# A decoder layer on one core: softmax weights of 4 of 50 key tiles made by VectorE as a base-2 polynomial, self masks moved to GpSimd

## Chip, core and metric

The kernel runs on one core of one Trainium2 chip. The metric is the device time of one launch, from the first to the last instruction of all engines, in microseconds (us). Several launches are timed and their median is taken; one more launch is run under the hardware profiler.

## What is computed

One pre-norm decoder layer in fp32: x has 1024 rows of 128, the context has 6404 rows of 96, there are 16 heads of 8 numbers each, and a mixture of 8 experts (2 chosen per row) at the end.

```
x = x + self_attention(layernorm(x))            # causal, 1024 keys, scale 1/sqrt(128)
x = x + cross_attention(layernorm(x), ctx)      # 6404 keys, no mask, scale 1/sqrt(8)
x = x + experts(layernorm(x))                   # 8 x (128->512->128), top 2 by a router
```

In each attention the weights are softmax(q k * scale), so every score needs one exponential: 16 heads x 1024 queries x 6404 keys in the cross attention, 105 million of them. Everything around the change is the making of these exponentials.

## The kernel before, in words

**Tiles.** Keys are taken in tiles of 128, queries in halves of 512, heads in four quads of four heads (lanes, r = 0 to 3). One PSUM bank holds the scores of one head, one key tile and one query half: 128 keys on the partitions, 512 queries. The cross attention has 8 units (2 halves x 4 quads); a unit has 50 key tiles of 4 banks, 200 banks, and a short tail of 4 keys per head whose exponentials are made once in `ptail`. So there are 1600 cross banks.

**Groups.** `score_groups` cuts the list of banks into groups; ScalarE turns a group into softmax numerators with one ACTIVATE (Exp) from PSUM to the slots of `probs` (15 slots of 512). In the self attention (48 groups) and the first 66 groups of the cross attention a group has 3 banks (PSUM banks 0 to 2, then 3 to 5; bank 6 is used for side work). From then on groups have 4 and 3 banks in turn (PSUM banks 0 to 3, then 4 to 6). The cross attention has 467 groups. PSUM is thus double-buffered: the scores of group g+2 go where those of group g lay.

**TensorE's order** is the loop in `attention` (L1252 on). For every group it waits until ScalarE has done the exponentials of that group, writes the scores of group g+2 (`score_group`, L1248), then sums every tile whose four banks are complete by group g: `sum_batch` (L1276) multiplies the weights of the four heads with the values, 4 matmuls of 512 columns that show as 8 in the trace since fp32 takes two passes. All sums of a unit go into PSUM bank 7. At the end of a unit the tail is summed (L1272), VectorE transposes the bank (L895), divides (L899, L902), and the first sum of the next unit waits for that transpose. The instructions of TensorE run in this order only.

**ScalarE's order** is `exponentials` (L659 on): for every group it waits for the scores of the group, and for the sums that still read the slots of `probs` that it will overwrite, then makes the exponentials (L665).

**VectorE** in the self attention multiplies each diagonal block of 128 x 128 weights by a 0/1 matrix `causal` (L916, 128 blocks in 29 of the 48 groups), after the exponentials of the group and before TensorE may sum them; `normalise` places the unit ends and the first half's projection and norm in the same order. In the cross attention after its first unit VectorE has only the unit ends.

**SyncE (SP)** loads key pieces into `k_ring` (five slots; 32 loads of 16 DMAs), each when its slot has been scored. Ahead of load five it issues the two 2 MB loads of the expert weights (L497, L498) into `w1_region` and `ctx_region`; TensorE waits for both at L1465, ahead of the first hidden units (L1499). **GpSimd** builds constants at the start and has one small matrix to build later (L578 to L587).

After the attention come projection, residual, norm, router, and the experts, whose order the change does not touch.

Of the kernel before, what the change touches and what calls it, by code (L numbers as in the profile page):

```python
# [6 lines left out]

# [8 lines left out]
I32 = mybir.dt.int32  # L16
# [29 lines left out]
CROSS_SCALE = float(HD) ** -0.5  # L46
EPS = 1e-5
# [56 lines left out]
def cross_plan():  # L104
    banks, batches = [], []
    for half in range(NHALF):
        for g in range(QUADS):
            for t in range(KT):
                at = len(banks)
                piece = (g, t, half, 0, HALF, 0)  # L110
                banks += [(r, [piece]) for r in range(LANES)]
                batches.append((g, half, t == 0, False, [(at + r, piece) for r in range(LANES)]))
            batches.append((g, half, False, True, None))
    return banks, batches


def score_groups(runs, slot):

    groups, at = [], 0
    for left, sizes in runs:  # L120
        n = 0
        while left:
            w = min(sizes[n % 2], left)
            slot = slot if slot + w <= SLOTS else 0
            groups.append((at, w, n % 2 * sizes[0], slot))
            slot, at, left, n = slot + w, at + w, left - w, n + 1
    return groups, slot


PLANS = (self_plan(), cross_plan())  # L130
SELF_GROUPS, NEXT_SLOT = score_groups(((len(PLANS[0][0]), (3, 3)),), 0)

BESIDE = 198
CROSS_GROUPS, _ = score_groups(((BESIDE, (3, 3)), (len(PLANS[1][0]) - BESIDE, (4, 3))), NEXT_SLOT)
GROUPS = (SELF_GROUPS, CROSS_GROUPS)
GROUP_OF = [[n for n, (_, w, _, _) in enumerate(groups) for _ in range(w)] for groups in GROUPS]
# [3 lines left out]
def n_groups(ph):  # L140
    return len(GROUPS[ph])


def place(ph, at):

    first, _, psum, slot = GROUPS[ph][GROUP_OF[ph][at]]
    return psum + at - first, slot + at - first


def before_in(ph, group, which):  # L150

    _, w, *at = GROUPS[ph][group]
    at = at[which - 2]
    return next((n for n in range(group - 1, -1, -1)
                 if GROUPS[ph][n][which] < at + w and at < GROUPS[ph][n][which] + GROUPS[ph][n][1]), None)


def batch_ready(ph, n):

    places = PLANS[ph][1][n][4] or PLANS[ph][1][n - 1][4]  # L160
    return GROUP_OF[ph][max(at for at, _ in places)]


def batches_through(ph, group):

    return 1 + max(n for n, b in enumerate(PLANS[ph][1])
                   if b[4] and any(GROUP_OF[ph][at] <= group for at, _ in b[4]))


def unit_ends(ph):  # L170

    return [(g, half, n + 1, batch_ready(ph, n)) for n, (g, half, _, last, _) in enumerate(PLANS[ph][1]) if last]


def diagonals(group):

    first, w, _, _ = GROUPS[0][group]
    return [(place(0, at)[1], col) for at in range(first, first + w) for _, t, half, q0, n, col in PLANS[0][0][at][1]
            if half * HALF + q0 == t * P]
# [37 lines left out]
def piece_scored(load):  # L217

    last = max(i for i, (_, ((g, t, half, *_),)) in enumerate(PLANS[1][0]) if load_of(half, g, t) == load)
    return GROUP_OF[1][last] + 1  # L220


def decoder_layer(nc, x, ctx, wqvk, wo_s, wq, bq, wk, bk, wv, bv, wo_x, bo, rw, rb, w1, b1, w2, b2, out):
    stack = ExitStack()
    with stack:
# [14 lines left out]
        w2_sb = ctx_region[:, 0:E * NF * D].rearrange("p (e f d) -> p e f d", e=E, f=NF)  # L240
        ctail = sb("ctail", [TAIL, C])
        w1_region = sb("w1_region", [P, E * FF])
        ctxT = w1_region[0:C + 1, 0:CT_RING * CHUNK * P].rearrange("p (r c) -> p r c", r=CT_RING)
        w1_sb = w1_region[:, :].rearrange("p (e f) -> p e f", e=E)
        ctailT = sb("ctailT", [C + 1, H, TAIL])
# [34 lines left out]
        causal = sb("causal", [P, P])  # L280
# [455 lines left out]
        def _(dve):  # L736
# [320 lines left out]
            for m in range(1, QUADS):  # L1057
                query_parts(m)
# [494 lines left out]
```

## Time and profile before

| what | value |
|---|---|
| timed runs, median | 1035.17 us (1035.10, 1035.17, 1039.96) |
| profiled execution, its own time | 1035.95 us |
| its span in the trace | 1034.2 us |
| mean granted TensorE clock | 0.975 |
| busy: PE, ACT, DVE, GpSimd | 887.2, 878.5, 173.0, 12.8 us |
| self attention, first to last group | about 73 to 157 us |
| cross attention | about 157 to 883 us |
| experts | about 906 us to the end |

The profiled execution is 0.8 us longer than the median of the timed runs; the span is 1.7 us shorter than its own time. The page is read in this order: the busy totals say which engines can be the bound at all; the chain that ended last says which of them alternate on the path; the groups and the timeline of a steady stretch say what a step of the loop costs and who waits for whom.

### The profile page before, as it was taken

What the parts mean: (1) busy time and instruction counts of PE and PEld (TensorE: products, weight loads), DVE (VectorE), ACT (ScalarE), POOL (GpSimd) and SP (SyncE); (2) the same over time, 40 slices, a digit from 0 to 9 for tenths busy, and PEclk for the clock granted to TensorE, in tenths of its full rate; (3) what the DMA queues carried; (4) which work ended last, traced back from release to release, by engine and by line L of the source; (5) the groups of instructions that cost most, each with busy time, mean ns of one, the idle gap of its engine ahead of it and who ended that gap; (6) DMA issues with size and microseconds to landing.
All of it is one profiled execution on the core that took longest, in us unless ns stands there. A gap on an engine that the chain in (4) does not pass through costs nothing.

```text
span 1034.2 us, 14948 instructions
## 1 busy us (share of the span) xinstructions
PE 887.2 (86%) x6144; PEld 260.8 (25%) x6144; DVE 173.0 (17%) x520; ACT 878.5 (85%) x682; POOL 12.8 (1%) x37
## 2 busy tenths in 40 slices
PE   6978889998888888888888888888888888499998
PEld 4552222221111211121111121111111111244443
DVE  5756643420000000000000000000000000522112
ACT  4656988999999999999999999999999999144443
POOL 3000000100000000000000000000000000000000
PEclk9986999999999999999999999999999999699999
DMA  4251007612211112211111211111120000000000
GB/s 138 85 194 44 1 3 119 171 31 45 48 37 32 34 35 43 47 40 31 31 35 34 48 47 34 32 31 34 44 46 7 1 1 1 2 1 0 1 0 21
DMA packets 19111, 42.12 MB, mean 41 GB/s; under 512 B 6130, under 2 KB 9308, under 8 KB 19036
## 3 DMA queue, kind: packets, MB, share of 16 engines
q1 hardware_dynamic: 19036, 41.09, 16.8%
q8 instruction: 51, 0.84, 0.3%
q14 instruction: 24, 0.20, 0.1%
HBM read 33.99 MB, written 7.08 MB: 40 GB/s over the span
## 4 chain that ended last, share of the span: by engine, by line
PE 32%; issue 32%; ACT 31%; DVE 4%; DMA 0%; ACTq 0%; DVEq 0%
ACT probs L665 31%; PE psum L1276 8%; PE psum L1510 6%; PE psum L1499 5%; PE psum L1248 5%; PE psum L1147 1%; PE psum L1181 1%; DVE turned L895 1%; PE psum L1185 1%; PE psum L1392 1%; PE psum L1272 1%; PE psum L1492 1%; DVE xn L768 1%; PE psum L1131 0%; PE psum L1378 0%
## 5 line engine op out<-in xcount | busy, mean ns | idle before, releaser
L665 ACT ACTIVATE probs<-psum 128x1536 f32<-128x1536 f32 (+1 forms) x515 | 782.5, 1838 | 30.9 <-PE psum L1248 19.6
L1276 PE MATMUL psum<-probs,v_ctx 128*9 128x512 f32 x3200 | 420.0, 597 | 2.8 <-DVE turned L895 2.8
L1248 PE MATMUL psum<-q_all,k_ring 32*128 32x512 f32 (+1 forms) x1792 | 262.3, 493 | 109.2 <-ACT probs L665 103.7
L1248 PEld LDWEIGHTS psum<-q_all,k_ring 32*128 32x128 f32 x1792 | 102.0, 185 | 505.4 <-ACT probs L665 462.8
L895 DVE STREAM_TRANSPOSE turned<-psum 128x512 f32<-128x512 f32 x16 | 11.5, 717 | 657.8 <-PE psum L1272 641.8
L719 ACT ACTIVATE probs<-psum,b_sb 128x512 f32<-128x512 f32 x64 | 44.0, 687 | 65.2 <-PE psum L1499 65.1
L1276 PEld LDWEIGHTS psum<-probs,v_ctx 128*9 128x9 f32 x3200 | 47.6, 88 | 103.6 <-issue 97.2
L1510 PE MATMUL psum<-probs,ctx_region 128*128 128x512 f32 x128 | 66.5, 604 | 0.0
L1499 PE MATMUL psum<-xnT,w_region 128*128 128x512 f32 x128 | 66.3, 601 | 0.0
L1276 PE MATMUL psum<-probs,v_self 128*9 128x512 f32 (+3 forms) x384 | 42.2, 541 | 2.9 <-DVE turned L895 1.5
L1499 PEld LDWEIGHTS psum<-xnT,w_region 128*128 128x128 f32 x128 | 24.3, 193 | 31.2 <-issue 27.8
L916 DVE TENSOR_TENSOR probs<-probs,causal 128x128 f32<-128x128 f32 x128 | 28.0, 285 | 17.2 <-ACT probs L665 16.6
L1510 PEld LDWEIGHTS psum<-probs,ctx_region 128*128 128x128 f32 x128 | 23.2, 189 | 27.3 <-issue 27.3
L1106 DVE SCALAR_TENSOR_TENSOR kparts_bc<-psum,b2T_sb,probs 128x512 f32<-128x512 f32 x14 | 10.5, 750 | 79.7 <-PE psum L1510 79.7
L1168 PE MATMUL psum<-ident,ctx_region 128*96 128x128 f32 x50 | 8.4, 297 | 10.1 <-DMA ctx_region<-in_ctx 8.6
L595 ACT ACTIVATE xnT<-psum 128x512 f32<-128x512 f32 x4 | 2.4, 597 | 16.9 <-PE psum L1122 16.8
L1122 PE MATMUL psum<-ident,xn 128*128 128x128 f32 x24 | 5.7, 383 | 12.2 <-DVE xn L768 12.2
L1185 PEld LDWEIGHTS psum<-wv_sb,w_region 97*128 97x128 f32 x100 | 14.1, 203 | 6.4 <-issue 6.3
L1181 PE MATMUL psum<-w_region,wk_sb 97*128 97x512 f32 (+1 forms) x26 | 14.2, 628 | 0.7 <-ACT w_region L595 0.7
L1185 PE MATMUL psum<-wv_sb,w_region 97*128 97x128 f32 x100 | 14.1, 286 | 0.0
L1147 PE MATMUL psum<-xnT,w_quads 128*128 128x512 f32 x32 | 13.9, 592 | 0.0
L595 ACT ACTIVATE turned<-psum 128x512 fp32r<-128x512 f32 x16 | 9.6, 599 | 4.1 <-PE psum L1147 4.1
(151 smaller groups left out, 287.1 us busy)
## 6 DMA issues: line engine op xcount, KB each, us to landing
k_ring<-kc_parts SPq DMA_DIRECT2D x256, 52.0 KB
k_ring<-kc_parts SPq DMA_DIRECT2D x256, 48.0 KB
kc_parts<-kparts_bc SPq DMA_DIRECT2D x8, 512.0 KB, 2.8
kc_parts<-probs SPq DMA_DIRECT2D x4, 512.0 KB, 2.8
w_region<-in_L_ffn_W SPq DMA_DIRECT2D x1, 2048.0 KB, 18.7
ctx_region<-in_ctx SPq DMA_DIRECT2D x1, 768.0 KB, 8.9
ctx_region<-in_ctx SPq DMA_DIRECT2D x1, 672.0 KB, 7.5
ctx_region<-in_ctx SPq DMA_DIRECT2D x1, 576.0 KB, 6.4
```

What stands on the lines that cost most here:

```text
L595: act.activation(dst, src, ACT.Copy).then_inc(done, n)
L665: act.activation(probs[:, slot:slot + w, :], psum[:, at:at + w, :], ACT.Exp, scale=SC[ph]).then_inc(L[ph]["exp_done"], 1)
L719: act.activation(hidden[:, n % FFN_RING, :], bank(n % 4), ACT.Relu, bias=b1_sb[:, e * NF + f:e * NF + f + 1]).then_inc(s["hid_relu"], 1)
L895: dve.transpose(turned[:, hf, :], bank(OUT_BANK)).then_inc(L[ph][f"turned{hf}"], 1)
L916: ins = dve.tensor_tensor(here, here, causal[:, :], ALU.mult)
L1147: pe.matmul(bank(QK_BANKS[m % 4]), quad_weight(which, g), xnT[:, hf * HALF:(hf + 1) * HALF], start=True, stop=True).then_inc(s["qkquad_ps" ...
L1181: pe.matmul(bank(2 + c % 2)[:, 0:w], wk_sb[:, :], ctxT[:, c % CT_RING, 0:w], start=True, stop=True).then_inc(s["kctx_ps"], 1)
L1185: mm = pe.matmul(bank(4 + c % 2)[:, t % CHUNK * D:(t % CHUNK + 1) * D], ctxT[:, c % CT_RING, at:at + P], wv_sb[:, :], start=True, stop=True)
L1248: mm = pe.matmul(into[:, col:col + n_q], keys, q_all[rows, g, hf * HALF + q0:hf * HALF + q0 + n_q], start=True, stop=True)
L1276: mm = pe.matmul(into[:, q0:q0 + w], v_all[:, h, t, :], probs[:, place(ph, at)[1], col:col + w], start=first, stop=last)
L1499: pe.matmul(bank(n % 4), w1_sb[:, e, f * P:(f + 1) * P], xnT[:, hf * HALF:(hf + 1) * HALF], start=True, stop=True).then_inc(s["hid_ps"], 1)
L1510: pe.matmul(bank(6 + m % 2), w2_sb[:, m % E, f, :], hidden[:, n % FFN_RING, :], start=(f == 0), stop=(f == NF - 1)).then_inc(s["hid_used"], 1)
```

## The change

- The queries are scaled by 1/sqrt(8)/ln 2 in the projection (weights and biases), so that a score s stands for 2^s; ScalarE's exponential then has the scale ln 2. This alters constants only.
- In cross units two to eight (numbers 1 to 7) the four banks of key tiles 2, 14, 26 and 38 are made by VectorE: 7 x 4 x 4 = 112 of the 1600 banks. Their scores take the last PSUM bank of a group, one such bank in each of four groups in a row; ScalarE makes the others of that group (3 or 2 instead of 4 or 3). The number of groups stays 467, and no group has more banks than before.
- `vector_tile` is new. For each of the four banks VectorE rounds the scores out of PSUM (adding 1.5 x 2^23) and subtracts them from the rounded number, which releases the PSUM bank; then 6 instructions over all 2048 columns build 2^n as an integer and multiply it with a polynomial of degree five. Each waits for the one before. The leading factor is put into a copy of the values (`vector_v`, four small instructions before unit one).
- TensorE must wait, before writing the scores of group g+2, until VectorE has taken the bank that lies there. The sum of a VectorE tile is placed 10 groups behind the group of its last bank (`VECTOR_LAG`), but never behind the last group of its unit, and waits for VectorE; VectorE overwrites its result only when the tile before has been summed.
- The self weights are masked in place by GpSimd's affine_select, one instruction for up to three neighbouring banks: 53 instructions for the 128 blocks, in the same 29 groups.
- The new tiles lie in `w1_region` and `ctx_region`, so SP loads the expert weights only after the last key load and after the sum of the last VectorE tile, which is in the last group of the last unit, just ahead of its tail.

```diff
+QUERY_SCALE = CROSS_SCALE / LN2
+ROUND = 1.5 * 2.0 ** 23
+VECTOR_TILES = (2, 14, 26, 38)
+VECTOR_LAG = 10
...
+def cross_groups(slot):
...
+        while half_full:
+            w = sizes[n % 2]
+            mine = 1 if waiting else 0
+            if len(half_full) < w - mine and not flush:
+                return
+            act = [half_full.pop(0) for _ in range(min(w - mine, len(half_full)))]
+            slot = slot if slot + len(act) <= SLOTS else 0
...
+            groups.append((here, n % 2 * sizes[0], slot, bool(mine)))
...
+            ready = max(group_of[r, g, t, half] for r in range(LANES))
+            order.append((ready + (VECTOR_LAG if vector else 0), t, vector))
+        last = max(ready for ready, t, vector in order if not vector)
+        order = sorted((min(ready, last), vector, t) for ready, t, vector in order)
...
@@ sync
-            sp.wait_ge(s["tail_done"], 1)
-            sp.wait_ge(s["vctx_done"], NCHUNK)
-            sp.dma_start(w1_sb, ...); sp.dma_start(w2_sb, ...)
             for load in range(PIECE_RING, LOADS):
                 sp.wait_ge(L[1]["qk_done"], piece_scored(load - PIECE_RING))
                 load_piece(load)
+            sp.wait_ge(L[1]["pv_batches"], vector_batch(*VECTOR_WORK[-1][0::3][:2]))
+            sp.dma_start(w1_sb, ...); sp.dma_start(w2_sb, ...)
@@ gpsimd
+            def mask_weights():
+                for group in MASKED_GROUPS:
+                    pool.wait_ge(L[0]["exp_done"], group + 1)
+                    for at, n, col in diagonals(group):
+                        here = probs[:, at:at + n, col:col + P]
+                        ins = pool.affine_select(out=here, in_=here, compare_op=ALU.is_ge, fill=0.0, base=0,
+                                                 pattern=[[0, n], [1, P]], channel_multiplier=-1)
+                    ins.then_inc(L[0]["masked"], 1)
@@ vector
+                def vector_tile(n):
+                    unit_no, g, half, t, groups = VECTOR_WORK[n]
+                    if n:
+                        dve.wait_ge(L[1]["made"], n)
+                    for r in range(LANES):
+                        scores = bank(GROUPS[1][groups[r]][1] + scalar_banks(1, groups[r]))
+                        dve.wait_ge(L[1]["qk_done"], groups[r] + 1)
+                        dve.tensor_scalar(vector_n[:, r, :], scores, ROUND, None, ALU.add).then_inc(L[1]["rounded"], 1)
+                        dve.wait_ge(L[1]["rounded"], n * LANES + r + 1)
+                        dve.scalar_tensor_tensor(vector_u[:, r, :], vector_n[:, r, :], ROUND, scores,
+                                                 ALU.subtract, ALU.subtract).then_inc(L[1]["taken"], 1)
...
+                    powered(dve.tensor_scalar(vector_n.bitcast(I32), vector_n, 127.0 - ROUND, 2.0 ** 23, ALU.add, ALU.mult))
+                    if n:
+                        before, _, _, t_before, _ = VECTOR_WORK[n - 1]
+                        dve.wait_ge(L[1]["pv_batches"], vector_batch(before, t_before))
+                    powered(dve.scalar_tensor_tensor(vector_p, vector_u, POWERS[4], vector_u, ALU.add, ALU.mult))
+                    for c in (3, 2, 1):
+                        powered(dve.scalar_tensor_tensor(vector_p, vector_p, POWERS[c], vector_u, ALU.add, ALU.mult))
+                    dve.scalar_tensor_tensor(vector_p, vector_p, POWERS[0], vector_n, ALU.add, ALU.mult)\
+                        .then_inc(L[1]["made"], 1)
...
-                        if group in MASKED_GROUPS:
-                            dve.wait_ge(L[0]["exp_done"], group + 1)
-                            for at, col in diagonals(group):
-                                here = probs[:, at, col:col + P]
-                                ins = dve.tensor_tensor(here, here, causal[:, :], ALU.mult)
-                            ins.then_inc(L[0]["masked"], 1)
...
@@ tensor
+                        if ph == 1 and taken_before(group + 2):
+                            pe.wait_ge(L[1]["taken"], taken_before(group + 2))
                         score_group(ph, group + 2)
...
+                        if ph == 1 and batches[n][6]:
+                            vector_sums += 1
+                            pe.wait_ge(L[1]["made"], vector_sums)
                         sum_batch(n)
```

## Rows read from the trace of the kernel before

**Rows 1.** The page: busy totals; the costliest group with its idle time before and releaser.

```profile
PE 887.2 (86%) x6144; PEld 260.8 (25%) x6144; DVE 173.0 (17%) x520; ACT 878.5 (85%) x682; POOL 12.8 (1%) x37
...
L665 ACT ACTIVATE probs<-psum 128x1536 f32<-128x1536 f32 (+1 forms) x515 | 782.5, 1838 | 30.9 <-PE psum L1248 19.6
```

**Rows 2.** Timeline, cross attention: start us, duration us, engine, line, operation, count, idle before.

```profile
442.03 0.50 PE L1248 MATMUL psum<-q_all,k_ring 32*128 32x512 f32 x4 [0.57 <-ACT probs L665]
...
442.47 1.04 PE L1276 MATMUL psum<-probs,v_ctx 128*9 128x512 f32 x8
...
443.44 0.51 PE L1248 MATMUL psum<-q_all,k_ring 32*128 32x512 f32 x3
...
445.14 0.51 PE L1248 MATMUL psum<-q_all,k_ring 32*128 32x512 f32 x4 [0.22 <-ACT probs L665]
```

**Rows 3.** Timeline: groups of three banks, first self groups; scores and the exponential after them.

```profile
74.08 6.82 ACT L665 ACTIVATE probs<-psum 128x1536 f32<-128x1536 f32 x5 [6.84 <-PE psum L1248]
...
177.23 0.50 PE L1248 MATMUL psum<-q_all,k_ring 32*128 32x512 f32 x3
...
177.78 1.45 ACT L665 ACTIVATE probs<-psum 128x1536 f32<-128x1536 f32 x1 [0.45 <-PE psum L1248]
```

**Rows 4.** Timeline, end of the first cross unit.

```profile
254.67 3.22 ACT L665 ACTIVATE probs<-psum 128x2048 f32<-128x2048 f32 x2 [0.70 <-PE psum L1248]
...
257.90 1.04 PE L1272 MATMUL psum<-ptail,v_ctx 128*9 128x512 f32 x8
...
259.08 0.72 DVE L895 STREAM_TRANSPOSE turned<-psum 128x512 f32<-128x512 f32 x1 [27.36 <-PE psum L1272]
...
259.85 1.05 PE L1276 MATMUL psum<-probs,v_ctx 128*9 128x512 f32 x8 [0.47 <-DVE turned L895]
```

**Rows 5.** Line L665 (exponentials): count, durations, first and last start.

```profile
L665 ACT ACTIVATE probs<-psum x515: 1443/1869/2508, 74.1 to 879.8; 128x1536 f32<-128x1536 f32 x105, 128x2048 f32<-128x2048 f32 x67
```

**Rows 6.** Groups by form on VectorE: count, busy us, mean ns of one, idle before.

```profile
L916 DVE TENSOR_TENSOR probs<-probs,causal 128x128 f32<-128x128 f32 x128 | 28.0, 285 | 17.2 <-ACT probs L665 16.6
...
L1109 DVE TENSOR_TENSOR turned<-turned,kparts_bc 128x512 f32<-128x512 f32 x14 | 9.7, 691 | 0.5
...
L804 DVE SCALAR_TENSOR_TENSOR q_all<-psum,low,turned 128x512 fp32r<-128x512 f32 x8 | 6.0, 751 | 7.5 <-ACT turned L595 6.8
...
L1068 DVE TENSOR_TENSOR x_sb<-x_sb,bo_rows 128x1024 f32<-128x1024 f32 x1 | 1.2, 1225 | 0.0
```

**Rows 7.** Timeline, self attention: masks behind a unit end.

```profile
86.66 2.11 DVE L916 TENSOR_TENSOR probs<-probs,causal 128x128 f32<-128x128 f32 x10
...
87.82 2.15 PE L1276 MATMUL psum<-probs,v_self 128*9 128x512 f32 x16 [1.39 <-DVE probs L916]
...
90.08 2.79 ACT L665 ACTIVATE probs<-psum 128x1536 f32<-128x1536 f32 x2 [4.31 <-PE psum L1276]
```

**Rows 8.** Stretch in the self attention: busy us by engine, granted clock, DMA share, GB/s.

```profile
85.00:100.00 15.00, 11.52 (x97) 4.14 (x97) 9.54 (x39) 8.54 (x7) 0.00 (x0) 0.66 0.09 22
```

**Rows 9.** GpSimd affine_select of 128 columns; a timeline of two of 1024 with VectorE beside.

```profile
L539 POOL TENSOR_SCALAR_AFFINE_SELECT causal<-causal 128x128 f32<-128x128 f32 x1 | 0.3, 312 | 0.1
...
183.01 2.32 POOL L580 TENSOR_SCALAR_AFFINE_SELECT v_self<-v_self 16x1024 f32<-16x1024 f32 x2
...
184.42 0.94 DVE L761 TENSOR_SCALAR rstd<-rstd 128x4 int32<-128x4 int32 x1
...
893.72 0.17 DVE L761 TENSOR_SCALAR rstd<-rstd 128x4 int32<-128x4 int32 x1
```

**Rows 10.** Load of w2, its landing; a stretch with it; timeline where the attention ends.

```profile
ctx_region<-in_L_ffn_W SPq DMA_DIRECT2D x1, 0.5 KB, 25.9
...
171.00:197.00 26.00, 25.12 (x178) 7.37 (x170) 10.59 (x34) 24.14 (x19) 3.12 (x3) 1.00 0.92 206
...
882.38 1.04 PE L1272 MATMUL psum<-ptail,v_ctx 128*9 128x512 f32 x8
...
906.13 2.31 PE L1499 MATMUL psum<-xnT,w_region 128*128 128x512 f32 x3
```

More of the change, by code:

```diff
@@ L133, with score_groups @@
-BESIDE = 198
-CROSS_GROUPS, _ = score_groups(((BESIDE, (3, 3)), (len(PLANS[1][0]) - BESIDE, (4, 3))), NEXT_SLOT)
+    units = [(half, g) for half in range(NHALF) for g in range(QUADS)]
+    return [(half, g, [(t, n > 0 and t in VECTOR_TILES) for t in range(KT)]) for n, (half, g) in enumerate(units)]
+def score_groups(banks, sizes, slot):
+    groups, at = [], 0
+    while at < len(banks):
+        w = min(sizes[len(groups) % 2], len(banks) - at)
+        slot = slot if slot + w <= SLOTS else 0
+        groups.append((banks[at:at + w], len(groups) % 2 * sizes[0], slot, False))
+        slot, at = slot + w, at + w
+    return groups, slot
@@ L141, in n_groups, with scalar_banks, slot_of, meets @@
     return len(GROUPS[ph])
-def place(ph, at):
-    first, _, psum, slot = GROUPS[ph][GROUP_OF[ph][at]]
-    return psum + at - first, slot + at - first
+def scalar_banks(ph, group):
+    here, _, _, vector = GROUPS[ph][group]
+    return len(here) - vector
+def slot_of(bank):
+    group = CROSS_GROUP_OF[bank]
+    here, _, slot, _ = CROSS_GROUPS[group]
+    return slot + here.index(bank)
+def meets(ph, a, b, which):
+    size = (lambda n: len(GROUPS[ph][n][0])) if which == 1 else (lambda n: scalar_banks(ph, n))
+    return GROUPS[ph][a][which] < GROUPS[ph][b][which] + size(b) and GROUPS[ph][b][which] < GROUPS[ph][a][which] + size(a)
@@ L150, in before_in, with taken_before @@
 def before_in(ph, group, which):
[L152 to L155, printed above, removed]
+    return next((n for n in range(group - 1, -1, -1) if meets(ph, n, group, which)), None)
+def taken_before(group):
+    return sum(CROSS_GROUPS[n][3] for n in range(1 + max([m for m in range(group) if meets(1, m, group, 1)], default=-1)))
 def batch_ready(ph, n):
-    places = PLANS[ph][1][n][4] or PLANS[ph][1][n - 1][4]
@@ L175, in diagonals @@
 def diagonals(group):
-    first, w, _, _ = GROUPS[0][group]
-    return [(place(0, at)[1], col) for at in range(first, first + w) for _, t, half, q0, n, col in PLANS[0][0][at][1]
-            if half * HALF + q0 == t * P]
+    here, _, slot, _ = GROUPS[0][group]
+    blocks = sorted((col, slot + i) for i, (_, pieces) in enumerate(here)
+                    for _, t, half, q0, n, col in pieces if half * HALF + q0 == t * P)
+    runs = []
+    for col, at in blocks:
+        if runs and runs[-1][2] == col and sum(runs[-1][:2]) == at:
+            runs[-1][1] += 1
+        else:
+            runs.append([at, 1, col])
@@ L182 @@
+    return runs
 MASKED_GROUPS = [g for g in range(n_groups(0)) if diagonals(g)]
```

189 lines of the change are left out of this document (129 added, 60 removed).

## The prediction

> **What bounds the kernel now.** The page comes first: ScalarE and TensorE are both busy for five sixths of the span, VectorE for a sixth, and the exponentials L665 wait only 30.9 us in all [rows 1]. They run from 74.1 to 879.8 us [rows 5], so ScalarE is the bound of 806 us of the 1034. Then a steady piece of the cross attention shows how close TensorE is behind. A pair of groups, 4 + 3 banks, takes 445.14 - 442.03 = 3.11 us [rows 2]. Five groups of three banks took 6.82 us, the last of them 1.45, so one takes 1.34 [rows 3]; four banks take 3.11 - 1.34 = 1.77. That is 0.427 us a bank and 0.063 a group. TensorE needs 0.43 for the scores of a group, whatever its size (442.03 to 442.47, [rows 2]), and 0.97 for the sum of a tile (8 matmuls, 442.47 to 443.44). A pair holds 7/4 tiles: 2 x 0.43 + 1.75 x 0.97 = 2.56 of 3.11 us. So TensorE has 0.55 us a pair to spare, and it can use it only two groups ahead, since PSUM holds two groups.
>
> **Step rules, from rows.** ScalarE frees itself 0.063 + 0.427 k after the start of a group of k banks; its record ends 0.17 + 0.427 k after it (1.45 for three), and the next engine starts 0.05 after a release (VectorE ends at 259.08 + 0.72, TensorE starts at 259.85, [rows 4]). Scores begun at 177.23 let the exponentials start at 177.78, 0.55 later [rows 3]. Stepping groups, scores, sums, slots and unit ends of the kernel before with these numbers gives 628.5 us from 254.67 [rows 4] to the end of the last tail sum; the trace has 882.38 + 0.97 - 254.67 = 628.7 [rows 4, 10]. The same steps are used for the change.
>
> **Cost 1, banks off ScalarE.** 112 banks x 0.427 = 47.8 us less. The count of groups, score writes and sums stays.
>
> **Cost 2, waits that take their place.** Fewer banks make ScalarE's groups shorter (1.34 and 0.92), while TensorE must do all sums, and those of the VectorE tiles in one lump. The lag of 10 groups puts that lump right beside the next VectorE tile, 13.7 groups on. One passage, groups 109 to 114 with 4, 2, 3, 2, 3, 3 banks for ScalarE, from the start of 109: TensorE sees its end at 1.93 and writes scores (0.43) and two sums, one of them the lagged tile 26 (1.95), until 4.31. Only then do the scores of group 112 start, so ScalarE starts it at 4.86, where its own work would be done at 1.77 + 0.92 + 1.34 = 4.03: 0.83 lost. TensorE sums one more (to 5.72), scores of 113 at 5.72, start at 6.27 against 4.86 + 0.92 = 5.78: 0.49 lost, and 0.07 at 114. 1.4 us lost, where four banks saved 1.7. Elsewhere a short group makes ScalarE reach a slot of `probs` before its sum is done: 0.44 a time, some 24 times. Stepped through groups 67 to 466, with a VectorE that costs nothing, waits for scores are 34 us and for slots 10, 44 in all; the kernel before has 3 by the same steps.
>
> **Cost 3, VectorE itself.** Rounding and subtraction read PSUM. A 128x512 instruction of two tensors takes 0.69, one with a column scalar 0.75 [rows 6]; neither shape here has a column scalar, so 0.69, ends 0.69 and 0.75. With 0.03 between, a bank takes 1.36, four 5.5. A step over 2048 columns: from 691 and 1225 ns for 512 and 1024 columns [rows 6] the slope is 1.04 ns a column, 2.29 us at 2048. Six of them with gaps: 13.9; a tile 19.4 us, against 44 x 0.427 + 13.7 x 0.063 = 19.6 of ScalarE alone between two tiles and about 21.3 with the waits above. So VectorE just fits. But the four banks of a tile come 1.12 us apart and are taken 1.36 apart, and TensorE may not write group g+2 before: stepped, this adds 8.6 us to ScalarE's path. `made` is never the last wait (15 groups, some 23 us, lie between the first bank and the sum, against 19.4).
> The bitcast step has one source in SBUF and runs over 2048 columns; no row shows it and I took the 2.29 above. The Trainium skill (VectorE: DVE Perf Modes, "The perf-mode tier table") gives fp32 `tensor_scalar` in SBUF double rate, 1.23 us at 2048; by it the tile is 18.3 us and the stepping 0.9 us shorter. No row here can tell.
> Cross attention together: waits 44 + 9 against 3 is +50, the banks -47.8, and the last lagged tile is summed after the last exponentials: +0.7. **+2.9 us.** Four `vector_v` instructions of 144 columns, 0.3 us each by L916's 0.285 at 128 [rows 6], run beside ScalarE in the first cross unit: 0; if not covered, 1.
>
> **Cost 4, masks.** VectorE's masks take 28.0 us [rows 6], behind unit ends too: ten of them end at 88.77 and TensorE waits 1.39 for them with ScalarE idle 4.31 [rows 7]. GpSimd's instruction costs 0.31 at 128 columns and 2.32 / 2 = 1.16 at 1024 [rows 9]: 0.95 ns a column. 53 x 0.31 us and the 16384 - 53 x 128 = 9600 further columns at 0.95 ns are 25.5 us, at most 1.3 in a group of 1.34, with no unit ends in the queue. In 85 to 100 the granted clock is 0.66 [rows 8], partly at 1.2 GHz after TensorE had idled; with the wait gone some of that should go. I take -3, between 0 (ScalarE waits on TensorE's half-rate sums anyway) and -6; if GpSimd is late instead, +3.
> Against it: while affine_select ran at 183.01 to 185.33, a VectorE instruction of 4 columns took 0.94 us [rows 9], where the same one takes 0.17 at 893.72. The Trainium skill (GPSIMD Engine Reference, "Key points") says that GpSimd shares its SBUF interfaces with VectorE, with contention for two-source or 2-port instructions; the row agrees. Eight unit ends in the self attention with 0.8 more each are 6 us of a queue that loses 28 us of masks: inside the +3.
>
> **Cost 5, expert weights.** They are now issued once the last VectorE tile is summed, 0.97 us before the tail sum's end E. The load of w2 took 25.9 us to land, beside key loads; 4.19 MB at the 206 GB/s of that stretch take 20.3 [rows 10]. The first hidden matmul comes 906.13 - 883.35 = 22.8 after E [rows 10]. Landing at E + 19.4 (hidden) or E + 25.0 (2.2 late). The keys are loaded by then, so 0; end +2.2. What is gained at 171 by taking the loads away is 0: no wait for keys shows there.
>
> **Sum.** 1035.95 of the profiled execution + 2.9 - 3 + 0 = 1035.9; the median of the runs lies 0.8 below. I forecast 1035.6.
>
> **Rivals.**
> A, the waits don't come: sums and scores keep ahead and ScalarE stays as full as before. 1035.95 - 47.8 - 3 = 985. Against it: the same step rules hit the kernel before within 0.3 us, and TensorE has only 0.55 us a pair to spare [rows 2]. Chance 0.06.
> B, they come by half (TensorE reorders a little, or the lump falls better): waits 25 instead of 50, 1011; with all between 985 and 1030: 0.22 for B. With A, faster by over 0.5%: 0.28. Half a percent, 5.2 us, is about what a measurement of this kernel can tell.
> C, slower: VectorE becomes the bound. Place: the wait for `taken` before scores. Decides where its tile passes about 20.5 us, as when a 2048-column step takes 2.5 instead of 2.29 (+4.2), or the PSUM pair 0.75 each (+4.1). At 2.9 a step (22.5 us a tile) a unit is VectorE's 4 x 22.5 + unit end, +36. For it: 19.4 against 19.6 leaves nothing; against it: all rows of VectorE lie on one slope. Both small ones, or one with the weights 2.2 late, give 1044 to 1047. Chance of slower by over 0.5%: 0.26.
> D, the change does nothing by itself: the last instruction is where it was since masks bring nothing and the cross part is even: 1037 to 1039, within the same case.
> Forecast, within 0.5%: 0.46, its own range 1030 to 1041.
> **Range.** Down to half of B's way, 1016; up to C's small ends together, 1048: 0.1 left out on each side.
>
> **What would show it.** The exponentials' idle before rises from 30.9 to about 80 us, released by L1248 in the main; VectorE's busy total rises by 28 x 19.4 - 28 = 515 us; TensorE shows double sums (x16) in the group before a VectorE tile, and short waits on VectorE before scores, 14 us in all. GpSimd rises by some 25 us. It is wrong if the idle before L665 stays under 50 us (A, B), if VectorE's 2048-column steps are not 2.29, or if TensorE waits for VectorE at sums (C).

## The result, and the profile after

The changed kernel takes 1053.40 us (median of 4 runs, 1048.44 to 1054.07), against 1037.57 us (1035.10 to 1041.96) for the kernel before on the same chip: ratio 1.0144, interval [1.0109, 1.0178] (the ratio is taken over all runs, so it need not be the quotient of the two medians). It is slower by 1.4%. The forecast was 1035.6 us, its range 1016 to 1048, so the result lies outside on the slow side. The profiled executions are 1035.95 and 1054.07 us, spans 1034.2 and 1052.3.

The page of the changed kernel: busy totals and the groups that matter (line, engine, operation, out<-in, count | busy us, mean ns | idle before, releaser).

```profile
PE 907.1 (86%) x6144; PEld 270.9 (26%) x6144; DVE 652.3 (62%) x788; ACT 840.7 (80%) x682; POOL 35.5 (3%) x88
...
L782 ACT ACTIVATE probs<-psum 128x1536 f32<-128x1536 f32 (+2 forms) x515 | 744.8, 1547 | 89.6 <-PE psum L1405 69.7
...
L1052 DVE SCALAR_TENSOR_TENSOR ctx_region<-ctx_region,w_region 128x2048 f32<-128x2048 f32 x84 | 192.5, 2292 | 2.9
L1033 DVE TENSOR_SCALAR w_region<-psum 128x512 f32<-128x512 f32 x112 | 77.2, 689 | 68.7 <-PE psum L1405 68.1
...
L1035 DVE SCALAR_TENSOR_TENSOR w_region<-w_region,psum 128x512 f32<-128x512 f32 x112 | 76.9, 687 | 3.8
...
L1046 DVE TENSOR_SCALAR w_region<-w_region 128x2048 int32<-128x2048 f32 x28 | 34.3, 1226 | 1.0
...
L686 POOL TENSOR_SCALAR_AFFINE_SELECT probs<-probs 128x384 f32<-128x384 f32 (+2 forms) x53 | 23.2, 459 | 120.0 <-ACT probs L782 119.9
```

Against [rows 1] the exponentials (now L782) fell from 782.5 to 744.8 us busy, and their idle time rose from 30.9 to 89.6. TensorE has the same 6144 matmuls and is busy 19.9 us longer: it does the same work more slowly. That is the row to be surprised by, and no step of the prediction allowed for it.

By stretches of the two traces, from the starts and ends of the exponentials:

| | before | after | |
|---|---|---|---|
| first exponential of the cross phase starts | 157.74 | 154.82 | -2.9 |
| group 67 of the cross phase (counted from 0) starts | 256.44 | 252.81 | -3.6 |
| from the end of group 67 to the end of the last (466) | 623.6 | 647.4 | +23.8 |
| from the start of the last to the end of the span | 154.4 | 151.7 | -2.7 |

The whole loss lies in the third row, called "the stretch" below; the rest gained 6.3 us. (The third row goes from end to end and the others by starts; the first and last of its exponentials changed in length, which is the 0.6 us that the rows lack of the 18.1 by which the span grew.) The step rules of the prediction give 623.6 us for it before, and 625.3 us after with the measured bitcast step. Some 22 us are not explained. These stepped figures, here and below, are worked out from the order of the program and the durations in the rows; no trace shows them.

Two things in the trace are not in those rules. The first, in the timeline of the changed kernel (start us, us, engine, line, operation, count, idle before). Left out are the records of SP and of weight loads:

```profile
604.92 0.73 PE L1405 MATMUL psum<-q_all,k_ring 32*128 32x512 f32 x3
...
605.58 1.04 PE L1440 MATMUL psum<-probs,v_ctx 128*9 128x512 f32 x8
...
606.55 0.73 PE L1405 MATMUL psum<-q_all,k_ring 32*128 32x512 f32 x4
...
607.21 1.05 PE L1440 MATMUL psum<-probs,v_ctx 128*9 128x512 f32 x8
```

The scores hold TensorE from 606.55 to 607.21 and from 604.92 to 605.58, 0.66 us; in [rows 2] it was 0.43 to 0.44 for three or four banks. A score matmul uses 32 rows of the array, those of its head. Before, a group holds consecutive banks and so three or four different heads. In the changed kernel VectorE's bank is the oldest one waiting, whatever its head, and in 72 groups it is of the same head as one of ScalarE's banks. The Trainium skill (TensorE: Matmul & The Clock Gate, "The mechanism" of its part on row and column tiling) says that a weight load overlaps matmuls in flight only where its row group is another one. The 0.66 against 0.44 agrees with it. So do the starts of the single matmuls. In a group of different heads the score matmuls start within 0.02 us of each other; where two are of one head, the last starts 0.31 to 0.54 us after the first, most often 0.34. That is so in 61 of the 72 groups, and in the other 11 the scores of the next group follow directly, so the two can't be told apart. Of the 395 groups without such a pair 5 show it too, all of them right behind the scores of another group. With 0.22 us more in each of the 72 groups the stepping gives 636.0 us in place of 625.3.

The second is the clock. Stretches of the changed kernel: us, busy us of PE, PEld, DVE, ACT and POOL with counts, granted clock, DMA share, GB/s; then the timeline of the middle one.

```profile
381.00:388.80 7.80, 5.54 (x46) 1.11 (x38) 7.70 (x4) 7.48 (x5) 0.00 (x0) 0.99 0.01 2
388.80:395.60 6.80, 6.56 (x31) 1.25 (x35) 3.29 (x3) 5.35 (x5) 0.00 (x0) 0.51 0.00 0
395.60:402.00 6.40, 6.39 (x54) 1.47 (x46) 4.75 (x8) 4.51 (x5) 0.00 (x0) 1.00 0.47 110
```

```profile
387.34 0.50 PE L1405 MATMUL psum<-q_all,k_ring 32*128 32x512 f32 x3
...
389.04 0.80 PE L1405 MATMUL psum<-q_all,k_ring 32*128 32x512 f32 x4 [1.20 <-ACT probs L782]
...
389.77 1.90 PE L1440 MATMUL psum<-probs,v_ctx 128*9 128x512 f32 x8
...
391.60 0.80 PE L1405 MATMUL psum<-q_all,k_ring 32*128 32x512 f32 x3
...
395.00 1.45 ACT L782 ACTIVATE probs<-psum 128x1536 f32<-128x1536 f32 x1 [1.11 <-PE psum L1405]
```

TensorE was busy 5.54 of 7.80 us and idle 1.20 at 389.04, waiting for ScalarE after a group without a tile to sum. From 388.8 the granted clock is 0.51, the 1.2 GHz level, for 6.8 us: scores take 0.73 (389.04 to 389.77) and a sum 1.83, and at 395.00 ScalarE has waited 1.11 us for scores. The pieces that begin in the stretch hold 40.8 us in the changed kernel and 6.8 us in the kernel before (at 416.2 and 641.4). If the 11.4 us that the stepping still lacks (647.4 - 636.0) belong to them, a microsecond at 1.2 GHz costs 0.28. That figure was fitted on this one trace, so the experiments had to test it.

### The profile page after: what moved, and what is told of

Read it like the earlier page. It is cut to its first block, busy times and chain, and to the rows that moved or that the text cites. A ratio compares the mean times of both kernels' runs of the same rounds, so it can differ in the third digit from the quotient of the medians.

```text
span 1052.3 us, 15703 instructions
## 1 busy us (share of the span) xinstructions
PE 907.1 (86%) x6144; PEld 270.9 (26%) x6144; DVE 652.3 (62%) x788; ACT 840.7 (80%) x682; POOL 35.5 (3%) x88
## 4 chain that ended last, share of the span: by engine, by line
PE 53%; ACT 24%; issue 15%; DVE 7%; DMA 0%; ACTq 0%; POOL 0%; DVEq 0%
ACT probs L782 24%; PE psum L1440 17%; PE psum L1405 12%; PE psum L1680 5%; PE psum L1669 5%; PE psum L1429 2%; PE psum L1437 2%; DVE w_region L1035 1%; PE psum L1298 1%; DVE w_region L1033 1%; PE psum L1332 1%; PE psum L1336 1%; PE psum L1562 1%; DVE turned L1012 1%; PE psum L1434 1%
## 5 line engine op out<-in xcount | busy, mean ns | idle before, releaser
L782 ACT ACTIVATE probs<-psum 128x1536 f32<-128x1536 f32 (+2 forms) x515 | 744.8, 1547 | 89.6 <-PE psum L1405 69.7
L1440 PE MATMUL psum<-probs,v_ctx 128*9 128x512 f32 x2976 | 401.6, 612 | 1.8 <-DVE turned L1012 1.3
L1405 PE MATMUL psum<-q_all,k_ring 32*128 32x512 f32 (+1 forms) x1792 | 275.7, 495 | 112.0 <-ACT probs L782 92.5
L1052 DVE SCALAR_TENSOR_TENSOR ctx_region<-ctx_region,w_region 128x2048 f32<-128x2048 f32 x84 | 192.5, 2292 | 2.9
L1033 DVE TENSOR_SCALAR w_region<-psum 128x512 f32<-128x512 f32 x112 | 77.2, 689 | 68.7 <-PE psum L1405 68.1
L1035 DVE SCALAR_TENSOR_TENSOR w_region<-w_region,psum 128x512 f32<-128x512 f32 x112 | 76.9, 687 | 3.8
L1050 DVE SCALAR_TENSOR_TENSOR ctx_region<-w_region 128x2048 f32<-128x2048 f32 x28 | 64.2, 2292 | 1.0
L1053 DVE SCALAR_TENSOR_TENSOR ctx_region<-ctx_region,w_region 128x2048 f32<-128x2048 f32 x28 | 64.2, 2292 | 1.0
L1046 DVE TENSOR_SCALAR w_region<-w_region 128x2048 int32<-128x2048 f32 x28 | 34.3, 1226 | 1.0
L1437 PE MATMUL psum<-ctx_region 128*9 128x512 f32 x224 | 30.4, 616 | 0.0
L686 POOL TENSOR_SCALAR_AFFINE_SELECT probs<-probs 128x384 f32<-128x384 f32 (+2 forms) x53 | 23.2, 459 | 120.0 <-ACT probs L782 119.9
```

The lines of the kernel that those rows point to most:

```text
L782: act.activation(probs[:, slot:slot + w, :], psum[:, at:at + w, :], ACT.Exp, scale=SC[ph]).then_inc(L[ph]["exp_done"], 1)
L1033: dve.tensor_scalar(vector_n[:, r, :], scores, ROUND, None, ALU.add).then_inc(L[1]["rounded"], 1)
L1035: dve.scalar_tensor_tensor(vector_u[:, r, :], vector_n[:, r, :], ROUND, scores, ALU.subtract, ALU.subtract).then_inc(L[1]["taken"], 1)
L1050: powered(dve.scalar_tensor_tensor(vector_p, vector_u, POWERS[4], vector_u, ALU.add, ALU.mult))
L1052: powered(dve.scalar_tensor_tensor(vector_p, vector_p, POWERS[c], vector_u, ALU.add, ALU.mult))
L1053: dve.scalar_tensor_tensor(vector_p, vector_p, POWERS[0], vector_n, ALU.add, ALU.mult)\
```

## The experiments

Theory: the loss is TensorE's. Half of it is score matmuls of one head that can't run side by side; the other half is the granted clock, which falls where the schedule leaves TensorE idle. Rivals: VectorE is the bound (its waits, or its long instructions beside the others), and the masks. For every run the table has the median, the ratio to the kernel before on the same chip (medians 1037.11 us beside e1 to e4, 1035.24 beside e5 to e8, 1036.28 beside e9 to e11) and, of its profiled execution, the length of the stretch, the us at 1.2 GHz in pieces that begin in it (w), what the stepping gives at full clock, and that plus 0.28 w.

| run | median us | ratio, interval | stretch | w | stepping | + 0.28 w |
|---|---|---|---|---|---|---|
| before | 1037.57 | | 623.6 | 6.8 | 623.6 | 625.5 |
| changed | 1053.40 | 1.0144 [1.0109, 1.0178] | 647.4 | 40.8 | 636.0 | 647.4 |
| e1 masks only | 1036.05 | 0.9991 [0.9969, 1.0013] | 623.6 | 6.8 | 623.6 | 625.5 |
| e2 no VectorE work | 1047.94 | 1.0086 [1.0051, 1.012] | 642.8 | 44.2 | 629.6 | 642.0 |
| e3 one wide step | 1051.97 | 1.0145 [1.0106, 1.0184] | 643.0 | 27.2 | 636.0 | 643.6 |
| e4 fill, two heads | 1060.84 | 1.0229 [1.0199, 1.0258] | 652.0 | 10.2 | 650.2 | 653.1 |
| e5 lane order | 1042.97 | 1.0064 [1.0039, 1.0089] | 630.2 | 13.6 | 627.5 | 631.3 |
| e6 empty group | 1035.85 | 0.9999 [0.9975, 1.0023] | 625.1 | 10.2 | 621.8 | 624.7 |
| e7 both, four tiles | 1016.72 | 0.9811 [0.9789, 0.9834] | 609.1 | 10.2 | 606.0 | 608.9 |
| e8 both, three tiles | 1013.59 | 0.9791 [0.9767, 0.9814] | 604.1 | 0 | 604.2 | 604.2 |
| e9 changed again | 1054.12 | 1.0185 [1.0155, 1.0215] | 640.8 | 17.0 | 636.0 | 640.8 |
| e10 lag alone | 1043.44 | 1.0041 [1.0004, 1.0078] | 633.3 | 23.8 | 625.4 | 632.1 |
| e11 fill, before | 1033.77 | 0.9984 [0.997, 0.9998] | 622.5 | 0 | 623.7 | 623.7 |

In all but the kernel before, e1 and e11, one more piece begins just ahead of the stretch and reaches some 1 us into it (4 in e5 and e10), which w leaves out. With it the last column stays within 2.3 us of the stretch in every row; without it, within 1.9.

**e1, the masks alone.** The kernel before, with the self weights masked by GpSimd.

```diff
-                                ins = dve.tensor_tensor(here, here, causal[:, :], ALU.mult)
+                        ins = pool.affine_select(out=here, in_=here, compare_op=ALU.is_ge, fill=0.0, base=0,
+                                                 pattern=[[0, n], [1, P]], channel_multiplier=-1)
```

> Only the masks are moved to GpSimd, in the kernel before; the cross attention is as before. The trace of the changed kernel starts its first cross group 2.8 us earlier than that of before (154.96 against 157.74). Expected 1035.95 - 2.8 = 1033. If GpSimd's masks gave nothing by themselves and the start came from something else, 1036; if they hurt elsewhere, 1038 or more.

The stretch is 623.6 us, as before, and the ratio's interval holds 1. The cross phase starts at 154.08 us in place of 157.74, but the first exponential of all was also 2.3 us earlier in this trace (71.8 against 74.1), which leaves 1.4. The masks have no part in the loss; what they bring is too small to tell.

**e2, no VectorE work.** VectorE fills its tile once and makes no weights, and TensorE no longer waits for banks to be taken; scores, sums and ScalarE's groups stay as in the changed kernel.

```diff
-                        dve.wait_ge(L[1]["qk_done"], groups[r] + 1)
-                        dve.tensor_scalar(vector_n[:, r, :], scores, ROUND, None, ALU.add).then_inc(L[1]["rounded"], 1)
...
+                    if n == 0:
+                        dve.memset(vector_p, 0.001).then_inc(L[1]["made"], 1)
...
-                            pe.wait_ge(L[1]["taken"], taken_before(group + 2))
```

> The changed kernel with VectorE's work on the 28 tiles left out (their weights are one constant, written once), and with it TensorE's waits for taken banks; scores, sums, groups and the order of TensorE stay. Theory clock and lumps: what costs the time is TensorE's own order and its drops to 1.2 GHz, so little comes back: the stepping gives 7.7 us less than with VectorE, so about 1046, still above the kernel before, and several 3.4 us stretches at 1.2 GHz stay. Theory VectorE is the bound: the 47.8 us taken off ScalarE show at last, about 990 to 1005.

The page of this kernel:

```profile
PE 906.0 (86%) x6144; PEld 268.2 (25%) x6144; DVE 147.3 (14%) x397; ACT 840.1 (80%) x682; POOL 35.6 (3%) x88
...
L782 ACT ACTIVATE probs<-psum 128x1536 f32<-128x1536 f32 (+2 forms) x515 | 744.2, 1549 | 88.3 <-PE psum L1379 68.5
```

VectorE has given up 505 us of work and the exponentials still wait 88.3 us. By the ratios, 1.0086 against 1.0144, the kernel is only 6.0 us faster than the changed one, near the 6.4 that the stepping puts on the waits for `taken` (636.0 - 629.6). Rival C of the prediction, VectorE as the bound, is out. The kernel stays slower than before for reasons that lie in TensorE. (Its profiled execution, 1056.79 us, from which the page and the row of the table are, is the slowest of its runs and has the lowest granted clock, 0.955; the ratio leaves it out, and the median of the other four is 1046.5.)

**e3, one wide step.** Of the six instructions over 2048 columns one is left, so the weights are not the softmax's.

```diff
-                    powered(dve.scalar_tensor_tensor(vector_p, vector_u, POWERS[4], vector_u, ALU.add, ALU.mult))
-                    for c in (3, 2, 1):
-                        powered(dve.scalar_tensor_tensor(vector_p, vector_p, POWERS[c], vector_u, ALU.add, ALU.mult))
-                    dve.scalar_tensor_tensor(vector_p, vector_p, POWERS[0], vector_n, ALU.add, ALU.mult)\
+                    dve.scalar_tensor_tensor(vector_p, vector_u, POWERS[0], vector_n, ALU.add, ALU.mult)\
```

> The changed kernel with one of the six instructions over 2048 columns per VectorE tile (the polynomial and the bitcast are left out); rounding, subtraction and all waits stay. The stepping has the long steps fully hidden at 1.23 + 5 x 2.29 us: same as the changed kernel within 3 us, 1050 to 1054. Theory VectorE is too full (18 us in a 21 us interval): 8 us or more less, 1045 or below.

The ratio is that of the changed kernel, 1.0145. VectorE's long instructions are hidden, and having them beside ScalarE and TensorE costs nothing that shows in intervals of 0.4%, 4 us, to either side.

**e4, filling the empty groups.** In each group with no tile to sum TensorE adds zeros for two heads.

```diff
+                    if ph == 1 and QUADS * 13 < n < len(batches) and batch_ready(ph, n) > done and not batches[n][2]:
+                        for r in range(2):
+                            pe.matmul(bank(OUT_BANK)[ROWS * r:ROWS * r + VC, :], v_ctx[H * TAIL:P, r, KT, :],
+                                      ptail[H * TAIL:P, 0:HALF], start=False, stop=False)
```

> The changed kernel plus work: in each of the 72 groups of units one to seven in which TensorE has no tile to sum, it multiplies zeros into the sums for two heads (0.49 us, nothing waits for it but TensorE's next group). Theory clock: the stretches at 1.2 GHz in the cross attention (44 us in all) vanish in the main, and with them 15 to 20 us: about 1036. By the stepping the added work alone costs 0.7 us. Theory that TensorE is simply short of time: slower, 1055 or more.

The forecast time missed by 25 us, on the wrong side. The timeline tells why:

```profile
402.51 1.03 PE L1462 MATMUL psum<-ptail,v_ctx 64*9 64x512 f32 x4
...
403.47 0.51 PE L1405 MATMUL psum<-q_all,k_ring 32*128 32x512 f32 x4
```

The fill of two heads holds TensorE 0.96 us, as long as the sum of four heads (0.97), where I had counted half. With 0.97 the stepping gives 650.2 and the trace 652.0. The clock part of the theory came out as hoped: 10.2 us at 1.2 GHz in place of 40.8, and in the mean of each execution a granted clock of 0.974 to 0.979 in the four of this kernel, against 0.955 to 0.972 in the eight of the changed kernel (e9's with them). The fill costs more than the clock gives back.

**e5, lane order.** VectorE's bank is taken from a head that the group's other banks don't use. VectorE takes the four in the order of their groups.

```diff
-                group_of[waiting[0]] = len(groups)
-                here.append(waiting.pop(0))
+                other = next((b for b in waiting if all(b[0] != o[0] for o in act)), waiting[0])
+                group_of[other] = len(groups)
+                here.append(waiting.pop(waiting.index(other)))
...
-                    for r in range(LANES):
+                    for at, r in enumerate(sorted(range(LANES), key=lambda r: groups[r])):
```

> Edit to the changed kernel: the VectorE bank of a group is taken, where there is one, from a head whose 32 rows of TensorE are not used by a ScalarE bank of the same group; groups in which two banks are of the same head fall from 72 to 16. Nothing is left out. Theory (score matmuls of one head can't run beside each other, 0.66 us for four banks where four different heads take 0.43): the stepping of the schedule gives the stretch from the 67th to the 466th group of the cross phase 627.5 us in place of 636.0, at full clock; with about as many half-clock stretches as the changed kernel has (11 us of cost), the run comes to 1043 to 1046 us and the page shows 638 to 640 us for this stretch. If the clock falls less often too, 1037 or better. Rival 1 (the loss is the clock and the empty groups alone): no change, 1052 to 1054. Rival 2 (each head's banks are wanted by VectorE in a new order, and TensorE's waits for VectorE grow by more than the 1 us of the stepping): up to 1050.

By the form of the instructions, the score matmuls of the changed kernel and of this one:

```profile
L1405 PE MATMUL psum<-q_all,k_ring 32*128 32x512 f32 x1696 | 269.9, 502 | 108.2 <-ACT probs L782 88.6 <-DVE w_region L1035 13.7 <-issue 4.3
```

```profile
L1406 PE MATMUL psum<-q_all,k_ring 32*128 32x512 f32 x1696 | 256.8, 498 | 109.4 <-ACT probs L783 87.2 <-DVE w_region L1036 16.1 <-issue 4.3
```

And the timeline of this one:

```profile
442.20 0.50 PE L1406 MATMUL psum<-q_all,k_ring 32*128 32x512 f32 x4 [1.11 <-DVE w_region L1036]
...
442.64 1.05 PE L1441 MATMUL psum<-probs,v_ctx 128*9 128x512 f32 x8
```

The same 1696 matmuls take 13.1 us less. Some 3 us of that are the clock, since this trace has 13.6 us at 1.2 GHz and that of the changed kernel 40.8: in e9, the changed kernel with 17.0, they take 266.8 us, 10.0 more than here. By 56 groups x 0.22 us it would be 12.3. A group of four with VectorE's bank in it holds TensorE 0.44 again (442.20 to 442.64). The ratio is 0.0080 lower than the changed kernel's, 8.3 us, where the stepping gives 8.5. The clock did not do it: four of the five executions, 1040.96 to 1043.19 us, have a granted clock of 0.963 to 0.965, where three of the changed kernel's four took 1053.21 to 1054.07 at 0.962 to 0.966. This settles the first half: reordering which head's bank goes into which group, with no work changed, removes most of it (16 such groups are left).

**e6, the sum in an empty group,** and **e10, the lag alone.** In e6 the lag is 8 groups and a VectorE tile's sum goes to the first group from there with no other tile. In e10 only the lag changes.

```diff
-VECTOR_LAG = 10
+VECTOR_LAG = 8
...
+        full = {ready for ready, t, vector in order if not vector}
+        last = max(full)
+        free = lambda ready: next(g for g in range(ready, last + 1) if g == last or g not in full)
+        order = [(free(min(ready, last)), t, vector) if vector else (ready, t, vector) for ready, t, vector in order]
```

> Edit to the changed kernel: the sum of a tile that VectorE made is put 8 groups behind its scores in place of 10, and then in the first group that has no other tile to sum. Groups with two sums fall from 24 to 4, groups with none from 74 to 54. Nothing is left out. Theory (the pair of an empty group, in which TensorE waits for ScalarE, and a double one, in which ScalarE waits for TensorE, is what costs, and an empty group is also where the granted clock falls): stepping 621.8 us for the 67th to the 466th group against 636.0 at full clock, and half-clock stretches fewer than 9; run 1032 to 1040. Rival 1 (double groups are hidden by the group held ahead): no change, 1050 to 1054. Rival 2 (lag 8 is too short and TensorE waits for VectorE's last step): idle of TensorE before the first matmuls of a VectorE tile of 1 us and more, 28 times, up to 1060.

> Edit to the changed kernel: the sum of a VectorE tile comes 8 groups behind its scores in place of 10, and nothing else; groups with two sums stay 24, groups with none 74, since 8 and 10 groups behind are the same place in the rhythm of the tiles. Nothing is left out. Theory of the stepping: 625.4 us at full clock in place of 636.0, so most of what the run with the empty-group placement gained (621.8) comes from the two groups alone, since the banks of GpSimd's and ScalarE's slots are held for less long; run 1036 to 1044. Rival (the gain of that run was the placement in empty groups): 634 to 636 at full clock, run 1048 to 1054.

Both came as the theory has it: 1035.85 and 1043.44 us, stretches 625.1 and 633.3. So the lag alone gives 10.6 us of the stepping, and the placement 3.6 more; by the ratios it is 10.7 and 4.4. The reason given for e10 was wrong in one point: the waits for slots of `probs` are 11.1 us in the stepping with either lag. What falls is the wait for scores, 51.5 to 41.0 us: there are 24 double sums with either lag, but with 10 groups 18 of them stand in the first group of the next VectorE tile or the one ahead of it, where ScalarE's groups are short; with 8 groups none does. e6 alone brings the time of the kernel before back, with 10.2 us at 1.2 GHz.

**e7 and e8, both edits.** Lane order and placement together, with tiles 4, 16, 28, 40 (e7) or 4, 20, 36 (e8).

```diff
-VECTOR_TILES = (2, 14, 26, 38)
+VECTOR_TILES = (4, 20, 36)
```

> Both edits of the two runs before in one kernel, and the VectorE tiles moved from 2, 14, 26, 38 to 4, 16, 28, 40 so that TensorE waits less for VectorE at a unit's first tiles. Nothing is left out. Theory: stepping 606.0 us for the 67th to the 466th group against 636.0 of the changed kernel and 623.6 of the kernel before; with half-clock stretches costing 3 to 11 us, the run comes to 1017 to 1026 us, 1 to 2% under the kernel before. Rival (ScalarE's time given away is returned elsewhere, whatever the order): no better than the kernel before, 1034 to 1040.

> The same two edits with three tiles per unit given to VectorE (4, 20, 36) in place of four. Nothing is left out. Theory: stepping 604.2 us for the 67th to the 466th group, 1.8 less than with four tiles, since TensorE is already the longer engine and a quarter of the groups with four banks gives back as much as it takes; run 1015 to 1025. Rival (more tiles on VectorE is always better, since ScalarE is the bound): 10 us longer than with four tiles, 28 x 4 x 0.427/4 = 12 us of ScalarE, so 1030 or so.

The page of e8:

```profile
L786 ACT ACTIVATE probs<-psum 128x1536 f32<-128x1536 f32 (+2 forms) x515 | 750.4, 1599 | 43.4 <-PE psum L1409 27.3
```

e7 is 1.9% and e8 2.1% faster than the kernel before. e8 forecast 604.2 us for the stretch and measured 604.1, with no half-clock piece that begins in it. Although it takes only 84 banks off ScalarE instead of 112, it is not slower than e7 (1013.59 against 1016.72; the intervals of the two ratios overlap): ScalarE's idle time is 43.4 us instead of the 56.5 on e7's page. The rival by which more tiles are always better forecast 1030 for it and falls. What moving the tiles within a unit gives by itself was not run.

**e9, the changed kernel again,** and **e11, the fill in the kernel before.** Both are for the clock. In e11 the fill is that of e4 with four heads, in the kernel before.

> The changed kernel itself, once more, to see how far the half-clock stretches move from one execution to another. In its first profile they took 40.8 us of the stretch from the 67th to the 466th group of the cross phase, which measured 647.4 us where the stepping at full clock gives 636.0. Theory (the difference is the clock, 0.28 us for each us at 1.2 GHz): the same sum, 636 + 0.28 x (us at 1.2 GHz), within 1.5 us, whatever their number is this time; with 20 to 40 us of them, 641.5 to 647. Rival (the difference is in the schedule and the clock only goes with it): 647 again, with more or fewer such stretches.

> Edit to the kernel before: in each group of the cross phase (from the second unit on) in which no tile is ready to be summed, TensorE sums zeros into the four heads, so that it is never left without work for a whole group; the result is unchanged. Theory (its granted clock falls where TensorE is least busy, 6.8 us of the stretch at 1.2 GHz, and this is worth 2 us): stepping 623.7 for the stretch against 623.6 without the fill, no half-clock stretch left, run 1034 to 1037, within 0.3% of the kernel before. Rival (the zeros delay the scores behind them): 10 us and more slower.

The whole stretch of the first profile and of e9, same columns as above:

```profile
254.69:902.13 647.44, 557.67 (x4244) 129.08 (x4244) 516.18 (x414) 584.45 (x399) 0.00 (x0) 0.97 0.14 31
```

```profile
255.22:896.03 640.81, 547.87 (x4244) 128.21 (x4244) 516.44 (x414) 583.34 (x400) 0.00 (x0) 0.99 0.15 31
```

This is one and the same kernel, with 40.8 and 17.0 us at 1.2 GHz, and 647.4 and 640.8 us of stretch: 6.6 us for 23.8, again 0.28. TensorE is busy 9.8 us less for the same 4244 matmuls while ScalarE's busy time is 1.1 us less. So the clock costs this much with the schedule unchanged. Taken off e9's stretch at this price it leaves 640.8 - 0.28 x 17.0 = 636.0 us, the figure of the stepping; so the schedule alone costs some 12 us against the 623.6 before. How much the clock adds varies from one execution to the next. The eight timed executions of the changed kernel (1047.99 to 1058.13 us, mean granted clock 0.972 down to 0.955, which is 59 to 95 us at 1.2 GHz) lie about a line of 0.27 us for each us, an estimate from clocks given to three digits. In e11 the half-clock pieces are gone, and the ratio is 0.9984 [0.997, 0.9998]: 1.1 us less of stretch for 6.8 us, a smaller price than 0.28 from this one pair of traces. But the price is not smaller in the kernel before: its 45 executions beside the experiments (1032.57 to 1041.87 us, granted clock 0.978 to 0.967) lie about a line of 0.35 us for each us (0.27 to 0.38 for each chip alone).

## Why the prediction was wrong

- **Cost 1, banks off ScalarE: -47.8.** The removed time was right in the stepping. On the page the busy total of the exponentials fell by 37.7 only, since a record is 0.11 us longer than 0.063 + 0.427 k (0.17 against 0.063): in a row of groups that overlaps with the next, in a group that stands alone it counts. In the traces 124 exponentials of the changed kernel have a gap behind them and 37 of the kernel before; these 87 more make 9.3 of the 10.1. The sentence after it is **the step that failed**: "The count of groups, score writes and sums stays." The counts stay, but not the time of a score write. "0.43 for the scores of a group, whatever its size" was read in groups of different heads and carried to groups with two banks of one head, where it is 0.66. In 72 groups that is 10.7 us of the stretch. The new function that deals out the banks, `cross_groups`, was in the diff; its effect on which heads meet in a group was never worked out.
- **Cost 2, waits in their place: +41.** The kind of wait was right. Forecast "about 80" us of idle time before the exponentials, measured 89.6 and, with less clock loss, 86.8. The passage with the lagged sum next to the next VectorE tile was a real cost: e10 takes it away with one number. The size was short because TensorE is slower than the rules had it. They also took full clock throughout, though the kernel before had 6.8 us at 1.2 GHz in the stretch, and Cost 4 itself reads the 0.66 of [rows 8] as what follows when TensorE has idled. The change adds idle groups; that the clock would follow was left out. This is the second step that failed, a term left at nothing without a reason. Cost: 11.4 us in the profiled execution, 4.8 in e9.
- **Cost 3, VectorE: +8.6 and 19.4 us a tile.** Right in kind: e2, without it, is 6.0 us faster than the changed kernel. TensorE waited 13.7 us for VectorE before scores, where 14 were forecast, and not for a finished tile (its sums, L1437, show no idle time before them). A tile takes 4 x 1.38 + 1.23 + 5 x 2.29 = 18.2 us busy. The bitcast step measured 1.226 us: my choice of 2.29 was wrong and the figure of the Trainium skill (VectorE: DVE Perf Modes, "The perf-mode tier table") was right. Rival C, VectorE the bound, had the right sign for a wrong reason: e2 and e3 show that it is not. (At 2.9 us a step its tile sums to 5.5 + 6 x 2.93 = 23.1 us, not 22.5.)
- **Cost 4, masks: -3.** The two profiles agree with it: the cross phase starts 2.9 us earlier, and in 85 to 100 us the granted clock is 0.89 in place of the 0.66 of [rows 8]. But it can't be called shown. In the same 15 us other profiles with GpSimd's masks have 0.50 (e6) to 1.00 (e3), and e11, with VectorE's, has 1.00. From the first exponential to the cross phase, profiles with GpSimd's masks took 79.8 (e3) to 85.0 us (e6), those with VectorE's 83.7 (before) and 80.4 (e11). The gain, if any, is within this scatter; a loss by late masks did not show. GpSimd's busy total rose by 22.7 us, 25 forecast.
- **Cost 5, expert weights: 0.** The landing of w2 took 16.1 us against 25.9 [rows 10], that of w1 10.0 with no key loads beside it. The first hidden matmul follows the end of the tail's sum by 925.00 - 904.87 = 20.1 us against 22.8: hidden, and 2.7 us better, for which I have no tested reason.
- **The sum.** Forecast +2.9 for the cross attention, measured +23.8 in the stretch. The forecast's own terms make +1.7 of it (625.3 - 623.6), the score writes 10.7 and the clock 11.4. That this closes at 647.4 proves little by itself, since the 11.4 were the remainder of this trace; what bears it out is that two executions of one kernel differ by the same 0.28. Both terms push the same way and neither was among the bounds, so the range's upper end of 1048 missed by 5.

## What to carry to other kernels

When work is dealt out anew among engines, check what each group of matmuls now holds, not only how many: with 32-row matmuls, two banks of one head in a group cost 0.22 us that four different heads don't. Here TensorE was within a fifth of ScalarE (2.56 of 3.11 us a pair), and taking banks off ScalarE paid only once TensorE was no longer left with an empty group and then a double one: the same 112 banks went from 1.4% slower to 1.9% faster (e7) by the order and the place of the tiles alone. And a stretch in which TensorE idles can cost twice, once for the wait and once at 1.2 GHz afterwards; since that part differs between executions of one kernel (4.8 and 11.4 us here), one profile is not enough to size it.

## What was not expected of the hardware

- Score matmuls of 32 rows on the same rows of the array: 0.66 us for a group with such a pair, 0.44 without.
- Each microsecond at 1.2 GHz cost 0.28 us in the changed kernel (0.27 by its eight timed executions), and one kernel had 40.8 or 17.0 us of them in two executions.
- A sum over two heads with 64 rows (4 matmul records) took 0.96 us, a sum over four heads with 128 rows (8 records) 0.97.
- With VectorE busy 62% of the span beside ScalarE and TensorE, taking away most of its long instructions changed nothing that shows (e3, ratio 1.0145 against 1.0144).
